# A three-part decoder layer on one core: the attention output turned by VectorE in 32x32 blocks, and the first three batches written out by hand

## What is computed

```python
# 1. linear attention, 32 heads of 8
q, k, v = relu(x @ qkv_weight.T)
vk   = [v, 1]^T k            # per head
y    = (vk q)[:8] / ((vk q)[8] + 1e-15)
x    = layernorm(x + y @ proj_weight.T + proj_bias)
# 2. cross attention to ctx, 16 heads of 16, rope over two coordinates in float16
q, k, v = rope(x @ Wq.T), rope(ctx @ Wk.T), ctx @ Wv.T
x    = layernorm(x + softmax(q k^T / 4) v @ Wo.T + bo)
# 3. low-rank feed-forward: 256 -> 64 -> 1024 -> 64 -> 256
x    = layernorm(x + gelu(x @ U1 @ V1 + b1) @ U2 @ V2 + b2)
```

## Time and profile before

| | us |
|---|---|
| median of three runs | 612.61 |
| the profiled execution: its time | 611.63 |
| the profiled execution: its span | 609.8 |
| TensorE busy | 531.0 (87%) |
| VectorE busy | 401.0 (66%) |
| ScalarE busy | 344.7 (57%) |
| GpSimd busy | 281.4 (46%) |

### The profile page before, as it was taken

How to read it: one execution, slowest core, us unless ns; L and a number is a source line. 1 busy time by engine, 2 the same in 40 slices (tenths; PEclk the granted TensorE clock), 3 DMA queues, 4 the chain that set the end, 5 groups by cost and what they waited for, 6 DMA issues and landing times.

```text
span 609.8 us, 11786 instructions
## 1 busy us (share of the span) xinstructions
PE 531.0 (87%) x4224; PEld 366.8 (60%) x4224; DVE 401.0 (66%) x906; ACT 344.7 (57%) x503; POOL 281.4 (46%) x321
## 2 busy tenths in 40 slices
PE   0763879999999999999999999999987777999993
PEld 0652656767676767767676767677654444555551
DVE  4431688786968787777869687877877532253534
ACT  4420236756665666657566656666565566546551
POOL 3608526255564556364554645562624222233324
PEclk9995999999999999999999999999979889999997
DMA  7750120120202020111202020201101002032322
GB/s 263 177 140 14 53 65 13 55 63 5 83 2 82 7 77 27 57 34 51 79 5 84 2 82 7 79 26 41 29 3 31 19 1 70 17 104 103 104 102 103
DMA packets 27209, 35.99 MB, mean 59 GB/s; under 512 B 5592, under 2 KB 13400, under 8 KB 27160
## 3 DMA queue, kind: packets, MB, share of 16 engines
q1 hardware_dynamic: 26440, 34.90, 18.4%
q10 hardware_dynamic: 720, 0.43, 0.3%
HBM read 23.51 MB, written 8.65 MB: 53 GB/s over the span
## 4 chain that ended last, share of the span: by engine, by line
PE 57%; DVE 15%; issue 14%; POOL 6%; ACT 5%; DMA 2%; SPq 1%; POOLq 0%; ACTq 0%
PE FR L1051 20%; PE BK L1219 7%; PE BK L1051 7%; DVE nmax L914 6%; PE SC L1177 5%; PE SC L1204 3%; PE FR L1133 3%; PE FR L1109 2%; PE FR L1264 2%; DVE lin_tm L834 2%; POOL rs L568 2%; PE BK L1236 2%; POOL c_fm L573 2%; DVE y L950 1%; DVE rden L830 1%
## 5 line engine op out<-in xcount | busy, mean ns | idle before, releaser
L914 DVE TENSOR_REDUCE nmax<-SC 128x4 f32<-128x1024 f32 x128 | 156.2, 1220 | 42.1 <-PE SC L1177 41.1
L680 ACT ACTIVATE probs<-SC 128x1024 f32<-128x1024 f32 x128 | 131.1, 1024 | 69.9 <-PE SC L1204 69.6
L1177 PE MATMUL SC<-k_blk,q_grp 48*128 48x512 f16 x256 | 51.0, 395 | 27.1 <-DVE nmax L914 18.0
L1219 PE MATMUL BK<-probs,v_aug 128*32 128x256 f32 x1024 | 69.9, 390 | 0.5 <-ACT probs L680 0.5
L479 POOL TENSOR_TENSOR att_fm_l<-att_raw,att_fm_h 128x512 fp32r<-128x512 f32 x16 | 20.5, 1283 | 76.5 <-ACT att_raw L656 76.5
L500 POOL TENSOR_TENSOR rs<-ve,minus_half 128x2 f32<-128x2 f32 x16 | 11.2, 701 | 94.6 <-DVE nm L956 94.6
L1204 PE MATMUL SC<-q_grp,k_blk 64*128 64x256 f16 x512 | 50.3, 275 | 3.4 <-ACT q_grp L638 1.6
L750 ACT ACTIVATE probs<-SC,b_ff 128x512 f32<-128x512 f32 x64 | 39.8, 687 | 22.5 <-PE SC L1370 21.7
L1177 PEld LDWEIGHTS SC<-k_blk,q_grp 48*128 48x128 f16 x256 | 12.4, 93 | 54.8 <-issue 22.6
L1051 PE MATMUL FR<-w_qkv_h,xs_fm_h 128*128 128x512 f32 x64 | 29.2, 456 | 16.6 <-POOL xs_fm_l L443 14.1
L1219 PEld LDWEIGHTS BK<-probs,v_aug 128*32 128x32 f32 x1024 | 26.8, 110 | 25.9 <-issue 14.2
(11 more groups left out here) (170 smaller groups left out, 1542.8 us busy)
## 6 DMA issues: line engine op xcount, KB each, us to landing
x_fm<-in_x_fm SPq DMA_DIRECT2D x16, 256.0 KB, 3.0
c_fm<-in_c_fm SPq DMA_DIRECT2D x16, 256.0 KB, 3.6
x_tm<-in_x_tm SPq DMA_DIRECT2D x16, 256.0 KB, 2.9
x_kept<-x2b SPq DMA_DIRECT2D x16, 256.0 KB, 2.3
x_tm<-x_kept SPq DMA_DIRECT2D x16, 256.0 KB, 2.8
out<-c_fm SPq DMA_DIRECT2D x16, 256.0 KB, 2.0
k_blk<-k_rope SPq DMA_DIRECT2D x128, 16.0 KB, 1.8
q_grp<-q_grp SPq DMA_DIRECT2D x32, 32.0 KB, 1.9
```

Source lines behind the costliest of these rows:

```text
L680: act.activation(probs[:, j % 4], SB[:], ACT.Exp, scale=SCALE).then_inc(s_exp, 1)
L914: dve.tensor_reduce(nmax[:, t, :, 2 * q:2 * q + 2], SA[:].rearrange("p (s f) t -> p s f t", s=2), AX.X, ALU.max, negate=True).then_inc(s_m ...
L1177: mm = pe.matmul(SA[:, 2 * s:2 * s + 2].rearrange("p h t -> p (h t)"), q_grp[n % NB][rows, q, t * P:(t + 1) * P], k_blk[n % NB][rows, q].r ...
L1219: mm = pe.matmul(BK[q // 2][HP * k:HP * (k + 1), (q % 2) * T:(q % 2 + 1) * T], v_aug[b % NB][:, t, HC * q + k], probs[:, j % 4, k], start= ...
```

## The change

**Attention output.** `ev_pv`, `o_t` and `att_t` go. VectorE transposes each half of the `pv` output straight from PSUM in blocks of 32x32 (`turn_pv`), which puts 32 tokens on 32 partitions and the features of one head on the free axis, four heads on the four partition groups. It takes one reciprocal and two multiplications there, and turns the result back with a third transpose into `att_raw`. ScalarE makes the high part from `att_raw` (one copy for two). The rows of `Wo` are permuted on the host to fit.

**Filling.** The steps -3 to -1 go. Their work is written out by hand on every engine, with the batches 0, 1 and 2 interleaved, and with SA, SB and both BK banks as further places for results. The first scores of batch 0 alternate between SA and SB. In SP's queue `x_fm(0)` comes ahead of the weights, the weights of the first block are loaded in two parts (keys and values first), and ScalarE's queue issues `c_fm(0)` and the weights of `k2` and `v2`.

**Small moves.** `add2(p)` stands ahead of `row_max 5`. After the last step `stats2(LAST-1)` stands behind `att_norm(LAST)`, and the interleaving with the first feed-forward block is another.

```diff
+            def turn_pv(b, half):
+                dve.wait_ge(s_pv_mm, NQ * b + NQ // 2 * (half + 1))
+                dve.transpose(o_tok[:, 2 * half:2 * half + 2].rearrange("p q b r -> p (q b r)"), BK[half][:]
+                              ).then_inc((s_pvc_ev, s_pvd_ev)[half], 1)
             def att_norm(p):
-                (two reciprocals 128x16 and two products 128x256, from FR[1] and BK[1])
+                dve.wait_ge(s_pvc_ev, p + 1)
+                dve.wait_ge(s_pvd_ev, p + 1)
+                dve.reciprocal(rden2[:], o_tok[:, :, :, D2]).then_inc(s_rden2, 1)
+                for half in range(2):
+                    part = slice(2 * half, 2 * half + 2)
+                    dve.tensor_tensor(out[:, :, :, half], o_tok[:, part, :, 0:D2],
+                                      rden2[:, part].unsqueeze(3).broadcast_to([P, 2, T // HP, D2]), ALU.mult
+                                      ).then_inc(s_att_ev, 1)
+                dve.wait_ge(s_att_ev, 2 * p + 2)
+                dve.transpose(flat(att_raw[:]), flat(lin_tm[:])).then_inc(s_att_raw, 1)
 # VectorE, step(b)
                 if on(n):
                     stats1(n)
+                if on(p):
+                    turn_pv(p, 1)
...
+                if on(p):
+                    add2(p)
                 if on(n1):
                     row_max(n1, 5)
-                if on(p):
-                    add2(p)
+                if on(b):
+                    turn_pv(b, 0)
                 if on(m):
                     lin(m)
 # TensorE, step(b): gone are o_t(p, 1), o_t(p, 0) and att_t(p)
 # TensorE, filling
+            kv1(0, 0, FR[1]); kv1(0, 1, FR[0]); q1(0); k2(0, SA0); v2(0, SA1)
+            vk(0, BK[1]); kv1(1, 0, SB0); lin(0, 0, FR[0]); lin(0, 1, FR[1]); kv1(1, 1, SB1); q1(1)
+            lin_t(0, SA0); vk(1, BK[1]); proj1(0, SA1); v2(1); lin(1, 0, FR[0]); lin(1, 1, FR[1])
+            kv1(2, 0, SB0); kv1(2, 1, SB1); lin_t(1, SA0); q1(2); x1_t(0); vk(2, BK[1]); proj1(1)
+            q2(0); lin(2, 0, BK[1]); lin(2, 1, BK[0]); k2(1)
+            scores1(0, 0); scores1(0, 1); lin_t(2, BK[1]); scores1(0, 2); x1_t(1, FR[1]); scores1(0, 3)
+            q2(1, BK[0]); scores1(0, 4); proj1(2); scores1(0, 5); scores1(0, 6); scores1(0, 7)
 # VectorE, end of the filling
+            stats1(1); rope_q(0); rope_q_sum(0); lin(2, (BK[1], BK[0])); row_max(0, 0); k_halves(1)
+            row_max(0, 1, SB); lint(2, BK[1]); ev_x1(1, FR[1]); row_max(0, 2); row_max(0, 3, SB)
+            rope_q(1); row_max(0, 4); rope_q_sum(1); row_max(0, 5, SB); row_max(0, 6); row_max(0, 7, SB); shift(0)
 # GpSimd, filling, after the first splits
+            rope_k(0); rstd1(0); residual_bias(1); residual2(0); split_x(3)
+            (low parts of w_v1 and w_d2)
+            rstd1(1); residual2(1); residual_bias(2); split_c(2); rope_k(1)
 # SP, filling, after the tables' first part
+            load_c(2); load_x_fm(3); load_x_tm(2); place_k(0); tables_in(2 * T, B * T, s_tab_in)
+            load_x_tm(3); place_q(0); place_k(1); place_q(1)
 # VectorE, end
-            stats2(LAST - 1)
-            att_norm(LAST)
+            turn_pv(LAST, 1)
+            att_norm(LAST)
+            stats2(LAST - 1)
             add2(LAST)
 # ScalarE, end
-            gelu(0, 2..3); ev_x2t(LAST - 1); gelu(0, 4); ev_p(LAST - 1); gelu(0, 5..7)
+            gelu(0, 2..5); ev_x2t(LAST - 1); gelu(0, 6); ev_p(LAST - 1); gelu(0, 7)
```

More of the change, by code:

```diff
@@ L387, in keep @@
                 sp.dma_start(a["x2"][q], x2b[:, q % 2]).then_inc(s_x2_out[q % 2], 16)
-            for b in range(FIRST, B):
-                if b >= -2 and on(b + 4):
+            load_c(2)
+            load_x_fm(3)
+            load_x_tm(2)
+            place_k(0)
+            tables_in(2 * T, B * T, s_tab_in)
+            load_x_tm(3)
+            place_q(0)
+            place_k(1)
+            place_q(1)
+            for b in range(B):
+                if on(b + 4):
                     load_x_fm(b + 4)
-                if b >= -1 and on(b + 3):
+                if on(b + 3):
                     load_c(b + 3)
[L394 to L397, removed]
+                if on(b + 2):
+                    place_k(b + 2)
                 if on(b - 2):
@@ L438, in split_in @@
                 pool.wait_ge(loaded[m % 2], 16 * (m // 2 + 1))
-                wait(pool, *used)
+                for done, count in used:
+                    wait(pool, done, count)
                 hi, lo, x = flat(dst[0][:]), flat(dst[1][:]), flat(src[:, m % 2])
@@ L548, in _ @@
                 pool.memset(q_grp[i][:].bitcast(F32), 0.0).then_inc(s_q_zeros, 1)
[L549 to L556 removed]
+            residual_bias(0)
+            split_x(1)
+            split_c(1)
+            split_x(2)
+            rope_k(0)
+            rstd1(0)
+            residual_bias(1)
+            residual2(0)
+            split_x(3)
+            for k in (V1, DD2):
+                pool.wait_ge(s_w_hi, k + 1)
+                src, hi, lo = split[k]
+                pool.tensor_tensor(lo, src, hi.bitcast(F32), ALU.subtract).then_inc(s_ff_lo, 1)
+            rstd1(1)
+            residual2(1)
+            residual_bias(2)
+            split_c(2)
+            rope_k(1)
+            for b in range(B):
                 step(b)
@@ L1012, in step @@
                     shift(n1)
-            for b in range(FIRST, B):
+            vk(0, BK[1])
+            weights_lo(P1)
+            lin(0)
+            k_halves(0)
+            weights_lo(Q2)
+            lint(0, SA0)
+            vk(1, BK[1])
+            add1(0, SA1)
+            stats1(0)
+            lin(1)
+            weights_lo(O2)
+            lint(1, SA0)
+            ev_x1(0)
+            vk(2, BK[1])
+            add1(1)
+            stats1(1)
+            rope_q(0)
+            rope_q_sum(0)
+            lin(2, (BK[1], BK[0]))
+            row_max(0, 0)
+            k_halves(1)
+            row_max(0, 1, SB)
+            lint(2, BK[1])
+            ev_x1(1, FR[1])
+            row_max(0, 2)
+            row_max(0, 3, SB)
+            rope_q(1)
+            row_max(0, 4)
+            rope_q_sum(1)
+            row_max(0, 5, SB)
+            row_max(0, 6)
+            row_max(0, 7, SB)
+            shift(0)
+            for b in range(B):
                 step(b)
@@ L1408, in _ @@
             h_ff(0, 1)
-            att_t(LAST)
             h_ff(0, 2)
```

464 lines of the change are left out of this document (247 added, 217 removed).

## The result

| | before | after |
|---|---|---|
| median, us | 613.13 (4 runs) | 625.76 (4 runs) |
| ratio | | 1.0215 [1.0162, 1.0268] |
| span of the profiled execution | 609.8 | 625.4 |
| first `shift_t` (end of the filling) | 84.22 | 81.06 |
| step 0 | 23.86 | 26.31 |

The forecast was 586. By the span, the filling gives 3.2 us instead of 19, step 0 costs 2.45 us instead of 0.5, the full steps cost 8.6 instead of giving 5.9, and the end costs 7.6.

The account below looks back on a forecast made before the run. TensorE was taken to bound the full steps, with a detour over VectorE, and waits the filling. Filling -19, steps 0 and 1 +0.5 -0.7, full steps -5.9, steps 13 to 15 -2.3 -1.4 -2.1, end +4.1: -26.8, 586 us (578 to 593).

Parts of the forecast that it names:

- End: Last part of the filling: chains on VectorE and GpSimd both end near 62, so `shift_t(0)` comes there instead of 84.2.
- Middle: Filling up to the first score chunk, near 46: TensorE's products set the time; the batch 0 keys, ready at 41, don't.
- tightest cover: Filling: `rstd1(0)` behind `rope_k(0)` at 34 to 35, wanted at 37; tables over 3 us later delay everything behind.
- The start: Beginning of the filling: with x ahead of part of the weights, TensorE starts at 11.8, 2.2 earlier.
- Rival A: Filling gives half, 9 instead of 19, as a transfer or GpSimd is late: 596 us; chance 0.18.
- The cost of the clock: Filling: light TensorE work between 46 and 62 brings half clock for `q2(1)` and step 0's first products; 3 us taken off.
- B: Rival, full steps: the transposes take 1.22 instead of 0.70, 1.4 a step for 14 steps, +20, 606 us; chance 0.06.
- D: Rival, slower: VectorE becomes the bound as a 32-bit PSUM transpose needs several passes; at 2.1 each, 643 us; chance 0.05.
- the turn in the detour: Full steps: `turn_pv(b, 0)` between `row_max 5` and `lin` adds 0.62 on the path, less 0.12 for `add2`: +0.50 a step.
- TensorE's release: Full steps: 1.47 a step removed from TensorE, of which 1.04 counts toward a shorter step.
- the products keep their size: Full steps, VectorE: reciprocals go from two to one, about -0.1, while the attention output's products take as long as before.
- The end: After the last `pv`: `stats2(LAST-1)` and GpSimd's work delay the last `x2_t` to 18.8 from 14.7, +4.1; step 15 gives -2.1.

Follow-up runs that it names:

- e5: Changed kernel with the old attention output and old end order, large rope tables issued from ScalarE's queue instead of SP's: 597.85 us, 0.9728 of before.
- e6: Changed kernel with the large part of the rope tables issued from ScalarE's queue instead of SP's: 613.34 us, 0.9975 of before.
- e4: Changed kernel with the large part of the rope tables issued behind `place_q(1)` in SP's queue: 617.96 us, 1.0054 of before.
- e1: Changed kernel with the attention output and end order of before, so the new filling only: 609.22 us, 0.9922 of before.
- e2: Kernel before with the new attention output alone, `stats2(LAST-1)` left ahead of the last turn: 621.88 us, 1.0116 of before.
- e13: e7 with GpSimd's `split_x(m + 1)` moved behind `keep_x2(q)`, nothing left out: 599.75 us, 0.9777 of before.
- e7: e6 with `stats2(LAST-1)` put back ahead of the last attention output's transposes: 610.47 us, 0.9930 of before.
- e10: e7 with GpSimd's `keep_x2(q)` moved between `split_x(m + 1)` and `att_lo(p)`: 615.98 us, 1.0048 of before.
- e11: e7 with VectorE's `rope_q_sum(n)` moved ahead of `row_max(n1, 6)`: 607.62 us, 0.9921 of before.
- e9: Kernel before with GpSimd's large two-operand operations cut to 16 columns, so the layer isn't computed: 601.98 us, 0.9788 of before.
- e3: Changed kernel with the large part of the rope tables issued right behind the first part in SP's queue: 619.38 us, 1.0077 of before.

## Why the prediction was wrong

**Filling, forecast -19, measured -3.2.** The step that failed is in "End": "The second chunk waits for `place_q(0)` ... some 3 us after the rope of the queries". I named `load_x_tm(3)` as what stands ahead of it in SP's queue, and not the two table transfers of 896 KB that stand ahead of that. e5 and e6, which start them earlier and from another queue, give back 9.5 and 10.1 us. The second step that failed is in "Middle": "the tables land near 30". That is when the last of the first part was issued (29.69 in after); its landing took 6.10 us more, which the sum had at nothing. The forecast calls this its tightest cover and names 33 as the sign: the tables landed at 35.8 in after and at 38.1 in e5. The chain leads from them over GpSimd's `k_rope` and `rstd1(0)` to the first scores, at 49.35 in after, 51.61 in e4 and 52.87 in e5 instead of 46. From there to `shift_t(0)` it is 17.8 us in e4 and in e5, where the forecast had 16 and 3 for the clock. The start (11.8 forecast, first product at 12.17 in after, 11.95 in e1) was right. Rival A had the mechanism, a late transfer, and too small a price.

**Step 0, forecast +0.5, measured +2.45.** The cost of the clock was put at `q2(1)` and the first products, and ended there. It reached into step 0, whose granted clock is 0.94 in after, 0.93 in e1 and 1.00 in before. The 16 us without work aren't needed for it: e5, where TensorE waits 3.3 us and not 16, has the same 25.28 us at 0.93 as e1 (25.30). Ahead of `shift_t(0)` TensorE is busy 7.05 of 10.66 us in e5, at a clock of 0.78. That this lighter work lowers the clock in step 0 isn't tested. The new output adds 0.94 (e2), for the 0.5 forecast. Step 1 was forecast at -0.7 and measured 0.0.

**Full steps, forecast -5.9, measured +8.6.** Transposes of 0.706 and 0.711 against 0.70: right, and B and D, which hang on their price, are out, though D's sign came true by another mechanism. The place of the turn in the detour was right too. The chain of before and that of e13 through the same part of a step:

```profile
282.77 1.41 PE FR L1051 x12
...
293.14 0.39 ACT p_fm L670
...
297.66 1.14 DVE nmax L914
```

```profile
295.48 0.61 ACT kv_tm L625
...
296.23 1.67 PE FR L1134 x12
...
300.06 0.61 ACT x_fm_h L670
...
306.67 0.39 ACT p_fm L680
...
311.66 1.14 DVE nmax L949
```

From `p_fm` to `row_max 6` it is 4.52 us before and 4.99 in e13, so +0.47 for the forecast +0.50. TensorE's release was over-sized at -1.04. With most of the stretching gone (e13) the step is 0.21 below before, so -0.68 is left of it, 0.36 a step or 4.0 us over eleven less than forecast. The chain of e13 shows what took its place, though not that it makes up the 0.36: ScalarE's eviction `kv_tm` stands where `o_t` was, those of `x_fm` where `att_t` was, and the twelve matmuls behind the first take 1.67 us where before has 1.41.

The larger part, 1.00 a step and 11.0 in all (28.72 to 27.72, e7 to e13), is the step that failed: "the products keep their size", and with them every other operation of VectorE that the sum didn't touch. They don't, once both operands are in SBUF and GpSimd works beside them. From e7 to e13 the pair of `att_norm` gives back 0.69, `q_sum` 0.92 and `q_cos` 0.66. e10 frees `q_cos` and `q_sin` and stretches the pair instead, and its step is longer; e11 frees `q_sum` alone, at a worse place, for 0.08. How the 1.00 divides between the pair, `q_sum` and `q_cos` isn't settled. The sign of it was in before's trace, a `q_sin` of 1.29 next to a `q_cos` of 0.45, the same operation on the same shape.

The Trainium skill (SBUF — State Buffer, SBUF: two separate sides) says that VectorE with two SBUF inputs and a GpSimd operation that reads SBUF exclude each other for the whole instruction. The trace agrees: 0.42 us alone, and an end 0.27 to 0.28 behind GpSimd's own end in after. I had read it and not applied it to an operand that moves from PSUM to SBUF.

**Steps 13 and 14, forecast -3.7, measured +0.1.** Between the runs these two move by 1 to 3 us with nothing changed in them (26.4 and 24.6 for step 13 in after and e6), so I read nothing from them. That forecast stays open.

**The end, forecast +4.1 less 2.1, measured +7.6.** The mechanism was right to 0.2 us at `att_lo`, and e7 shows that the order costs 4.7. Mis-sized was what follows: `wo` and `x2_t` run slow after the wait, as TensorE idles 3.03 us and its clock is 0.86, so that 22.3 us pass instead of 18.8. Not all of the 7.6 is explained: e1, with the old output and its order, already ends 1.4 us later than before.

Of the versions that do all the work, e5 (new filling, old output) is the fastest at 597.85, 0.9728 of before, with e13 (both parts of the change, with three orders mended) level within the intervals at 0.9777.

## What to carry to other kernels

Follow a small transfer's wait through everything that its queue holds ahead of it, with sizes: two table loads of 896 KB held a 64 KB placement for 16 us, and 256 KB loads for 18 to 21 where they stood elsewhere in the queue. Issued early from another engine they were through before the placement came; what ran beside them was still slowed, 10.3 us for a load that takes 2.9 alone. Add the time to landing, not only the time to issue: 6 us of it were left out for the tables' first part. When you cut one cost, look at which of the others were counted as fixed. When an operand of VectorE moves from PSUM to SBUF, or VectorE's work shifts in time, look at what GpSimd does at that moment and at what waits behind the operation; moving one GpSimd pair was worth 11 us over eleven steps, moving another operation by total stretch alone lost 6. A large gap between the shortest and the mean duration of one shape in the trace is the sign of it.

## What the runs showed of the hardware

- A float32 transpose in 32x32 blocks on VectorE, 128x512, takes 0.706 us from PSUM to SBUF and 0.711 within SBUF.
- A float16 product or sum of 128x512 on VectorE takes 0.41 to 0.42 us alone and up to 1.49 beside GpSimd. A GpSimd instruction with one tile as input does it too: the old `q_sum` stays at 0.78 beside a high part of 0.62 when the two-operand ones are thin (e9). GpSimd's own operation is stretched less (`k_rope` 1.16, and 1.44 in e13).
- Reading the tables back, 2 x 896 KB spread over the partitions, held up what was behind it in its queue for 15.9 to 20.6 us in after, e3 and e4. A 256 KB load issued at 38 landed after 18.2 us behind them in the same queue (e3), 10.3 beside them in the other (e6), and 2.9 without them (e4).
